# A macaron block on 8 cores: phase 2 of the FFN moved from two engines to one, and issued two steps at a time

## The reference

```python
x = x + 0.5 * ffn(layernorm(x))      # gate: argmax over 8 experts; x + expert(x) of the chosen one
x = x + attn(layernorm(x))           # 16 heads of 64, rotary, window of 128 tokens to each side
x = x + 0.5 * ffn(layernorm(x))
...
scores = einsum('bsh,eh->bse', x, gate_w)
onehot = one_hot(argmax(scores, axis=-1), 8)
expert_out = einsum('bsh,efh->bsef', x, expert_w)
return x + einsum('bsef,bse->bsf', expert_out, onehot)
```

## Time and profile before

| | us |
|---|---|
| median of the two runs | 2561.74 |
| the two runs | 2532.72, 2590.76 |
| the profiled execution | 2537.4 |
| its span, slowest core (4) | 2535.8 |
| spans of the eight cores | 2516.0 to 2535.8 |

### The profile page before, as it was taken

One profiled execution on the slowest core, in us unless ns is written; L12 is line 12 of the kernel. 1 busy time (PEld: TensorE's weight loads), 2 busy tenths in 40 slices (PEclk: granted clock), 3 DMA queues, 4 the chain that ended last, 5 costly groups with the idle time before them and its releaser, 6 DMA issues.

```text
span 2535.8 us, 27915 instructions; the slowest of 8 cores (2516.0 to 2535.8 us)
## 1 busy us (share of the span) xinstructions
PE 2053.3 (81%) x9872; PEld 1032.3 (41%) x9872; DVE 843.0 (33%) x1704; ACT 447.2 (18%) x1059; POOL 380.8 (15%) x511
## 2 busy tenths in 40 slices
PE   3685778998987389968977996899595989898983
PEld 0662324443446143423433442434491434343462
DVE  2103104242333443345234424533303232424242
ACT  3200000000000116513740461165400000000000
POOL 0000112323335100000000000000000114141443
PEclk9557989999999595678568657956655999999997
DMA  7006996546556651012001100100001445545565
GB/s 197 0 1 128 199 208 162 167 125 149 150 144 197 139 133 40 1 39 101 1 34 67 40 1 34 67 1 12 31 1 51 154 145 151 150 150 138 158 198 201
DMA packets 78117, 257.60 MB, mean 102 GB/s; under 512 B 9232, under 2 KB 20496, under 8 KB 73888
## 3 DMA queue, kind: packets, MB, share of 16 engines
q0 software_dynamic: 57648, 203.28, 30.3%
q1 hardware_dynamic: 20336, 52.55, 7.4%
HBM read 249.27 MB, written 33.63 MB: 112 GB/s over the span
## 4 chain that ended last, share of the span: by engine, by line
PE 74%; DMA 10%; DVE 8%; issue 3%; ACT 2%; POOL 1%; SPq 0%; DVEq 0%; POOLq 0%; ACTq 0%
PE pdf L93 35%; PE pss L93 11%; PE pq L93 5%; PE pgf L93 5%; PE pspt L98 4%; DMA webuff<-wexpT 4%; PE pv L93 4%; PE pbf L93 3%; PE pso L93 2%; DMA webuff<-wexp_bf 2%; DMA wexp_bf<-webuff 2%; DMA x_sb<-xT 2%; PE pba L93 1%; DVE xc_at L104 1%; DVE qraw_at L104 1%
## 5 line engine op out<-in xcount | busy, mean ns | idle before, releaser
L93 PE MATMUL pdf<-lmbuff,webuff 128*128 128x512 bf16 (+1 forms) x5120 | 1037.7, 366 | 131.6 <-DVE lmbuff L104 78.6
L93 PEld LDWEIGHTS pdf<-lmbuff,webuff 128*128 128x128 bf16 x5120 | 507.6, 100 | 661.6 <-issue 186.3
L104 DVE TENSOR_TENSOR lmbuff<-xcf,mkbuff 128x1024 bf16<-128x1024 bf16 (+1 forms) x320 | 210.3, 667 | 667.5 <-PE pdf L93 653.1
L150 POOL DMA_DIRECT2D webuff<-wexp_bf x288 | 154.5, 537 | 979.7 <-PE pdf L93 810.0
L125 ACT CAST ev8f<-pdf 128x1024 bf16<-128x1024 f32 (+1 forms) x20 | 17.6, 930 | 1397.9 <-PE pdf L93 1397.9
L111 DVE TENSOR_SCALAR pn_bf_at<-p_at,rc_at 128x384 bf16<-128x384 f32 x256 | 95.9, 417 | 240.3 <-PE pspt L98 233.0
L141 ACT ACTIVATE p_at<-pss,negc_at 128x384 f32<-128x384 f32 x256 | 147.8, 590 | 36.0 <-PE pss L93 35.5
L93 PE MATMUL pss<-biasq_sb,idb 128*128 128x384 bf16 x256 | 128.5, 502 | 15.3 <-DVE k_sb_at L104 15.3
L93 PE MATMUL pss<-k_sb_at,q_sb_at 64*128 64x384 bf16 x256 | 127.5, 498 | 0.0
L93 PE MATMUL pgf<-gwT_sb,x_sb 128*128 128x8 f32 x576 | 123.2, 361 | 0.0
L93 PEld LDWEIGHTS pgf<-gwT_sb,x_sb 128*128 128x128 f32 x576 | 123.0, 333 | 0.0
(11 more groups left out here) (120 smaller groups left out, 1526.4 us busy)
## 6 DMA issues: line engine op xcount, KB each, us to landing
webuff<-wexp_bf POOLq DMA_DIRECT2D x288, 512.0 KB, 5.2
webuff<-wexpT POOLq DMA_DIRECT2D x32, 512.0 KB, 15.8
wexp_bf<-webuff SPq DMA_DIRECT2D x32, 512.0 KB, 10.7
wbufA_at<-wqkv_bf POOLq DMA_DIRECT2D x6, 2048.0 KB, 9.5
wbufB_at<-wqkv_bf POOLq DMA_DIRECT2D x6, 2048.0 KB, 9.0
x_sb<-xT SPq DMA_DIRECT2D x8, 1152.0 KB, 22.7
mkbuff<-onehot_sc SPq DMA_DIRECT2D x64, 128.0 KB, 6.6
outT<-x_sb SPq DMA_DIRECT2D x8, 1024.0 KB, 12.2
```

What stands on the lines that cost most here:

```text
L93: E.matmul(a, b, c, start=st, stop=sp, tile_position=tp),
L104: eng, lambda E, o=out, x=a0, y=a1, op=op: E.tensor_tensor(o, x, y, op),
L150: eng, lambda E, o=out, i=in_: E.dma_start(o, i), inc=sem, n=16)
```

## The change

Phase 2 runs wholly on VectorE, with the two halves of the scratch used in turn. In the experts 0 to 3 two steps are popped instead of one, so the eight steps are through after expert 3. The mask loads for the next chunk are emitted at expert 2 instead of 0, and `gen_xc` at expert 4 instead of 2.

```diff
             def emit_phase2_d(d, t0, w, p1cnt, p1acnt):
-                eng = "dve" if d < 4 else "pool"
-                sl_ = 0 if d < 4 else 1
+                eng = "dve"
+                sl_ = d % 2
                 us = uscr[:, sl_ * 512: sl_ * 512 + w]
...
                     if pending:
                         cc, eng = pending.pop(0)()
                         ph2[eng] = cc
-                    if e == 0 and ti + 1 < len(tcs):
+                    if e < 4 and pending:
+                        cc, eng = pending.pop(0)()
+                        ph2[eng] = cc
+                    if e == 2 and ti + 1 < len(tcs):
                         b.wait("sp", "dve", lm_last[(ti + 1) % 2])
                         mk_next = load_masks(ti + 1, tcs[ti + 1][0],
                                              tcs[ti + 1][1])
-                    if e == 2 and ti + 1 < len(tcs):
+                    if e == 4 and ti + 1 < len(tcs):
                         xc_next = gen_xc(ti + 1, tcs[ti + 1][0], tcs[ti + 1][1])
```

## The result

| | before | changed |
|---|---|---|
| median | 2536.69 us (10 runs) | 2555.89 us (11 runs) |
| profiled execution | 2537.4 us | 2546.97 us |
| its span, slowest core | 2535.8 us (core 4) | 2545.4 us (core 3) |

The changed kernel is slower: ratio to before 1.0073, 95% interval 1.0055 to 1.0092, which is +14 to +23 us, +18.5 in the middle. In some executions of either kernel the cores of a die (four of the eight) ran at a lower granted clock and took 30 to 60 us longer; the ratio leaves these out, and the 2590.76 us beside the prediction is, by its time, one of them. So the median of 2561.74 us stood too high, and ten runs give 2536.69. The two profiled executions differ by 9.6 us, less than the ratio says.

A forecast was written before the change was run, and what follows sets the result against it. It took TensorE (81% busy) and its uncovered stops, short chunks, tails and first-FFN start as what counts: 25.6 - 15 + 6.4 - 1.5 + 0 = +15.5 us on 2537.4, so 2552.9 us; range 2536 to 2584.

The forecast's parts named there:

- Sum: Whole kernel: terms total +15.5 us on the profiled execution's 2537.4 us, giving 2552.9 us; bounds +9.7 to +47.2.
- The stop: Between chunks: a second phase-2 step ahead of the first lmbuf adds 3.2 us at eight stops, +25.6 us.
- The clock's term: After each stop between chunks: TensorE's low clock might last longer; bounds 0 to +7 us, taken 0.
- The short chunk: Last 256-column chunk of each FFN: without GpSimd steps, waits for weight loads shrink; taken -15 us, bounds -19.2 and +4.2.
- The lateness of VectorE in the experts 0 to 3: Short chunk: two steps and four lmbuf take 7.8 us against TensorE's 7.15; charged 2 us in both chunks together.
- The tail: After each FFN's last chunk: 32 instructions on VectorE alone take 17.0 us, not 13.8; +6.4 us in all.
- The start: Start of the first FFN: eight mask loads now stand behind weight copies; bounds -3.1 to +4, taken -1.5 us.
- Rival 1: Short chunk: first halves tighten too and all 19.2 us come back; +5.5, 2543 us; chance 0.12.
- Rival 2: Short chunk: slower weight loads make it wait throughout; 2584 us, 2591 with clock; chance 0.08 shared with longer low clock.
- Rival 3: Stops between chunks are not lengthened, because ScalarE's evictions or a load end them; 2527 us; chance 0.03.
- its own first term: Stops between chunks: one more step ahead of the first lmbuf costs 3.2 us each, +25.6 us over eight.

The follow-up runs named there:

- x2_short_only: Kernel before, with only the four GpSimd phase-2 steps popped in the short chunk moved to VectorE, one per expert; 2519.55 us, ratio 0.9933.
- x8_double_keep_pool: Kernel before, with VectorE's four steps popped two at a time at experts 0 and 1, GpSimd's four left at experts 4 to 7; ratio 1.0097.
- x1_one_step: Changed kernel with the second pop taken out: one phase-2 step per expert, experts 0 to 7, all on VectorE; 2523.86 us, ratio 0.9953 to before.
- x3_start_only: Kernel before, with only the mask loads moved from expert 0 to 2 and the centring from 2 to 4; 2534.77 us, ratio 0.9994.
- x4_no_step_e0: Changed kernel with no step at expert 0, two at expert 1, one at experts 2 to 7, tail shared with GpSimd; 2485.51 us, ratio 0.9791 to before.

## Why the prediction was right and where it was wrong

*What was wrong: the base of the time.* The working was a difference, +15.5 us, on the profiled execution's 2537.4 us, and the measured difference is +18.5 us (14 to 23). But the time given, 2552.9 us, stands below the 2561.74 us that was the median of before at that time, so as a pair of times the forecast says "faster by 9 us", while every step of it says "slower by 15". The step that failed is the one under "Sum": it saw that the two runs lay 58 us apart and that a like pair after the change would read up to 2577, and did not draw the conclusion in the time. What the runs showed in its place: ten runs put the base at 2536.69 us, 25 us below that median, and the changed kernel is slower than it by 0.73%, not faster. That 2552.9 us stands so near the measured 2555.89 is owed to the profiled execution, which happened to lie within 1 us of this base. Where a base is two runs that far apart, the forecast is the difference, and it has to be put on the same base as the comparison. The size of the change, the range (2536 to 2584 us, measured 2555.89) and the sign of the sum held. The stages of the profiled pair add up to +13.2 us, so that 15.5 lies nearer to 18.5 is no merit of the terms.

*The stop, +25.6 us.* Right: +3.14 us at each of eight stops on every core, by the one step that stands there. The dose confirms it: 0, 1, 2 and 4 steps ahead of the first lmbuf give 3.03, 6.3, 9.5 and 15.84 us. The clock's term, taken 0 with up to 7: right within 0.1 us a chunk, the full chunks stay at 113.0 after 6.3 and 9.5 and are 113.1 after 15.84 us.

*The short chunk, -15 us.* Right in its place and cause, with -16.8 measured: x2_short_only has the gain without the longer stop, x8_double_keep_pool the longer stop without the gain. Second halves of 30.9 and 29.0 us stand where some 29.6 were expected. The lateness of VectorE in the experts 0 to 3 was charged 2 us in both chunks together; TensorE's timeline shows a wait of 1.02 us on a phase-2 step, and against x1_one_step the two chunks differ by 0.7 and -0.2 us: if anything, it was less than charged.

*The tail, +6.4 us.* Right, with +6.1 measured: 32 instructions of 0.42 us at a pitch of 0.53. By the rule of the Trainium skill (SBUF — State Buffer, "Who interferes with whom") an instruction of VectorE with two SBUF inputs contends with an instruction of GpSimd that reads SBUF; 0.76 us beside it and 0.42 without it agree.

*The start, -1.5 us.* Not shown: x3_start_only is 0.9994 (0.9982 to 1.0005), and the first chunk varies by more than the term.

*The rivals.* Rival 1, that more than the second halves comes back: the first halves moved by -0.7 and +0.7 us on the cores shown, so it didn't occur. The prediction's reason against it, that GpSimd did not compute in the first halves, misreads, which give GpSimd 13.06 us there: its first step already stands in the first half. It is right for the waits all the same, since the first FFN's longest wait in that half comes ahead of the step. TensorE's and GpSimd's timelines of before:

```profile
764.93 14.16 PE L93 MATMUL pdf<-lmbuff,webuff 128*128 128x256 bf16 x128 [1.70 <-DMA webuff<-wexp_bf]
771.41 1.28 POOL L104 TENSOR_TENSOR uscrf<-x_sb,mbf 128x512 f32<-128x512 f32 x1
```

Rival 2, that loads turn into the wait of the short chunk: the loads landed sooner, not later. Tile webuff over the last chunks of the second FFN, to set beside the earlier trace rows:

```profile
L150 POOL DMA_DIRECT2D webuff<-wexp_bf x63: 528/528/531, 2300.6 to 2495.0; - x63
DMA to landing us min/median/max: 4.1/4.8/6.4
```

The same page of the Trainium skill, in the same section, infers that two-input instructions of VectorE do not hold up GpSimd's descriptor writes; with 128 more of them in the chunks, beside the loads, issues of 0.53 us and landings of 4.8 us agree. Rival 3, that stops are not lengthened, fell with the first of them.

*What the prediction did not price* was the other direction of its own first term: it found that a step ahead of the first lmbuf costs 3.2 us and did not ask what the step already there costs. Taking it away, and every step at expert 0 with it, brings the stop from 6.3 to 3.0 us and is worth more than all the rest of the change: x4_no_step_e0 is at 0.979 where x1_one_step is at 0.995, 6 us of the difference being its shared tail.

## What to carry to other kernels

When an engine's queue is shared by a chunk's evictions, background work and the first operand of the next chunk, the order at that one place counts and the busy shares don't: one background step of 3.2 us ahead of the operand costs 3.2 us at every boundary, and the same step behind it shows no cost. Background work in the queue that issues loads is free while the prefetch lead is longer than the work and the landing of a load together, and expensive once it isn't: here 5.4 + 5.2 us against a lead of 14 us in a full chunk and of 7 us in the short one. So look at the shortest chunk. And before an edit is judged, take its parts by themselves: here a gain of 17 us was hidden under a loss of 25.

## What was not expected of the hardware

TensorE's clock after a stop does not follow the stop's length smoothly. After 6.3, 9.5 and 15.8 us the full chunks take nearly the same, 113.0 to 113.1 us in the mean, and none of 48 kept the clock; after 3.2 us 15 of 48 kept it and 33 lost it, for 3.4 us as a rule and 5.4 us in the case shown; after 1.48 us 41 of 48 kept it and seven lost it for 3.4 us. So the clock was worth 1 us a chunk in x4_no_step_e0, in steps rather than by degrees: a longer stop loses it more often, and hardly for longer. What decides between the two cases at one length of stop was not tried.
